# Inverse roots of the variances in the later projections: one power operation on GpSimd for ScalarE's root and VectorE's reciprocal

## What is computed

```python
def layer_norm(x, w, b, eps):
    mu = jnp.mean(x, axis=-1, keepdims=True)
    var = jnp.var(x, axis=-1, keepdims=True)
    return (x - mu) * jax.lax.rsqrt(var + eps) * w + b

xn = layer_norm(group_norm(x), w_in, b_in, eps)      # eps 1e-5, in layer 3 1e-6
p = (xn @ W_value + b_value) * sigmoid(xn @ W_gate + b_gate)
# layers 2 and 3 also: gate = sigmoid(xn @ W_ogate + b_ogate), stored for the end of the layer
```

## Time and profile before

| | before |
|---|---|
| median of 3 runs | 1588.93 us (1588.11 to 1591.24) |
| the profiled execution | 1591.19 us, of which the span is 1589.4 us |
| PE busy | 1357.7 us (85%) |
| DVE busy | 1217.4 us (77%) |
| ACT busy | 978.3 us (62%) |
| POOL busy | 447.3 us (28%) |
| L910, reciprocal, DVE | 12 of 3.35 us |
| L826, root, ACT | 12 of 0.72 us |
| table loads in the projections, ACT | 5 of 1.28 us (L843 2, L830 2, L836 1) |

### The profile page before, as it was taken

One profiled execution on the slowest core, in us unless ns is written; L12 is line 12 of the kernel. 1 busy time (PEld: TensorE's weight loads), 2 busy tenths in 40 slices (PEclk: granted clock), 3 DMA queues, 4 the chain that ended last, 5 costly groups with the idle time before them and its releaser, 6 DMA issues. The chain is left out here.

```text
span 1589.4 us, 26467 instructions
## 1 busy us (share of the span) xinstructions
PE 1357.7 (85%) x9025; PEld 750.7 (47%) x9025; DVE 1217.4 (77%) x2069; ACT 978.3 (62%) x1578; POOL 447.3 (28%) x387
## 2 busy tenths in 40 slices
PE   5767797878796997799979998898889979995987
PEld 5516332222583442345559997222245537772443
DVE  5644787699699886789957777997689968997664
ACT  4675588634344787677846665356768856662555
POOL 5400397320000893310000000685320000002665
PEclk9898898999898998999989999898999989996999
DMA  9368210056785220489988886794168989996998
GB/s 352 121 193 298 92 54 1 1 160 199 257 291 199 94 80 1 144 293 342 339 314 305 302 305 229 273 375 173 38 267 343 345 326 382 418 401 212 381 392 313
DMA packets 152692, 381.60 MB, mean 240 GB/s; under 512 B 15728, under 2 KB 15984, under 8 KB 152432
## 3 DMA queue, kind: packets, MB, share of 16 engines
q1 hardware_dynamic: 140176, 356.64, 61.8%
q10 hardware_dynamic: 12384, 23.28, 3.9%
HBM read 191.11 MB, written 188.74 MB: 239 GB/s over the span
## 5 line engine op out<-in xcount | busy, mean ns | idle before, releaser
L1162 PE MATMUL banks<-work 128*128 128x256 f32 x1408 | 335.5, 386 | 21.8 <-DVE work L1233 11.9
L1162 PEld LDWEIGHTS banks<-work 128*128 128x128 f32 x1408 | 262.3, 195 | 68.5 <-issue 16.7
L714 PE MATMUL banks<-work,w 64*64 64x512 f32 x2048 | 265.4, 609 | 12.5 <-DVE work L941 9.7
L1514 POOL TENSOR_TENSOR xT<-xT,work 128x512 f32<-128x512 f32 x192 | 241.0, 1271 | 60.0 <-DVE work L1563 56.6
L941 DVE SCALAR_TENSOR_TENSOR work<-banks,bias,work 128x512 f32<-128x512 f32 x256 | 188.5, 748 | 39.7 <-PE banks L714 33.0
L830 ACT ACTIVATE work<-banks,bias 128x512 f32<-128x512 f32 x256 | 171.7, 685 | 57.8 <-PE banks L714 57.7
L1192 ACT COPY work<-banks 128x512 f32<-128x512 f32 x176 | 103.1, 586 | 145.2 <-PE banks L1162 141.6
L714 PEld LDWEIGHTS banks<-work,w 64*64 64x64 f32 x2048 | 105.0, 135 | 129.7 <-DVE work L941 80.2
L1331 POOL MEMSET work<- 32x2048 bf16 x4 | 7.2, 1799 | 563.6 <-issue 466.7
L1259 DVE TENSOR_TENSOR work<-work 128x512 f32<-128x512 f32 x176 | 120.9, 687 | 58.3 <-ACT work L1192 57.2
L1563 DVE SCALAR_TENSOR_TENSOR work<-banks,bias,work 128x512 f32<-128x512 f32 x192 | 141.9, 747 | 30.2 <-ACT work L1488 15.1
(11 more groups left out here) (168 smaller groups left out, 2161.9 us busy)
## 6 DMA issues: line engine op xcount, KB each, us to landing
hidden_rows<-work SPq DMA_DIRECT2D x128, 512.0 KB, 4.0
work<-hidden_rows SPq DMA_DIRECT2D x120, 512.0 KB, 6.8
products<-work SPq DMA_DIRECT2D x88, 512.0 KB, 4.0
work<-products SPq DMA_DIRECT2D x88, 512.0 KB, 5.0
work<-gate_rows SPq DMA_DIRECT2D x64, 512.0 KB, 5.7
work<-hidden SPq DMA_DIRECT2D x40, 512.0 KB, 6.1
work<-in_x SPq DMA_DIRECT2D x32, 512.0 KB, 4.7
gate_rows<-work SPq DMA_DIRECT2D x32, 512.0 KB, 3.3
```

Of the source, the lines that this page charges most:

```text
L714: mm = pe.matmul(out[side, :], w(name)[rows, side], h[rows, t % H, :], start=True, stop=True)
L1162: mm = pe.matmul(ZB[c % 2][:, r * N:r * N + N], a[:, kk, rows_of(r, c)], x[:, kk, :], start=(kk == 0), stop=(kk == 1))
L1514: pool.tensor_tensor(columns(t), columns(t), term[:, t % RING, :], ALU.add).then_inc(x_sb, 1)
```

## The change

For each set, ACT's root and DVE's reciprocal are left out. The epsilon is added on DVE together with the clipping at zero (L905), and GpSimd raises the result to the power -0.5 with one `tensor_tensor` of 128x512, whose second input is the column of -0.5 read again for each column. GpSimd waits for the variance and for its own split of the set before. The dummy root that loads the table is left out too. The same holds for layers 1, 2 and 3. Left out of the diff below are the lines that drop the semaphore `sd_sb`.

```diff
--- before.py
+++ after.py
@@ -821,10 +821,6 @@
-            def root(x):
-                act.wait_ge(var_sb, 2 * x + 2)
-                nc.scalar.activation(sd[:, x % 2, :], sd[:, x % 2, :], ACT.Sqrt, bias=eps).then_inc(sd_sb, 1)
-
@@ -840,19 +836,14 @@
-            nc.scalar.activation(core.fold[:, 14:15], core.cols[:, 0:1], ACT.Sqrt)
             act.wait_ge(norm.gmean_in, 1)
             for u in range(PAIRS):
                 for x in range(SETS_OF_ROOTS - 2):
                     if u == 2 * last_step(x) + 4:
                         square_of_mean(x)
-                    if u == 2 * last_step(x) + 7:
-                        root(x)
                 squares(u)
             for x in (SETS_OF_ROOTS - 2, SETS_OF_ROOTS - 1):
                 square_of_mean(x)
-            for x in (SETS_OF_ROOTS - 2, SETS_OF_ROOTS - 1):
-                root(x)
@@ -876,6 +867,9 @@
             for x in range(SETS_OF_ROOTS):
                 rest = sd[:, x % 2, :]
+                pool.wait_ge(var_sb, 2 * x + 2)
+                at_least(pool, split, 4 * x)
+                pool.tensor_tensor(rec, rest, core.cols[:, 2:3].broadcast_to([P, T]), ALU.pow).then_inc(rec_sb, 1)
                 pool.wait_ge(rec_sb, x + 1)
                 pool.tensor_scalar(high[:, 0, :], rec, later[0], None, ALU.mult).then_inc(split, 1)
@@ -902,12 +896,7 @@
                 dve.wait_ge(var_sb, 2 * x + 1)
-                dve.tensor_scalar(var, var, 0.0, None, ALU.max).then_inc(var_sb, 1)
-
-            def inverse(x):
-                dve.wait_ge(sd_sb, x + 1)
-                at_least(dve, split, 4 * x)
-                dve.reciprocal(rec, sd[:, x % 2, :]).then_inc(rec_sb, 1)
+                dve.tensor_scalar(var, var, 0.0, eps, ALU.max, ALU.add).then_inc(var_sb, 1)
@@ -954,8 +943,6 @@
                     if u == 2 * last_step(x) + 5:
                         variance(x)
-                    if u == 2 * last_step(x) + 8:
-                        inverse(x)
                 squares(u)
@@ -978,8 +965,6 @@
-                if u in (2, 4):
-                    inverse(SETS_OF_ROOTS - 3 + u // 2)
```

More of the change, by code:

```diff
@@ L694, in project @@
         norm = GroupNorm(core, layer, f"proj{layer}", [n for n in (gate_w, value_w, ogate_w) if n], sums_w)
-        (sq_a, sq_v, sum_mm, mean_sb, var_sb, sd_sb, rec_sb, split, fac_mm, h_sb, gate_mm, val_mm, gate_sb,
-         val_sb) = core.sems(f"proj{layer}", "sq_a sq_v sum_mm mean_sb var_sb sd_sb rec_sb split fac_mm h_sb gate_mm "
+        (sq_a, sq_v, sum_mm, mean_sb, var_sb, rec_sb, split, fac_mm, h_sb, gate_mm, val_mm, gate_sb,
+         val_sb) = core.sems(f"proj{layer}", "sq_a sq_v sum_mm mean_sb var_sb rec_sb split fac_mm h_sb gate_mm "
                              "val_mm gate_sb val_sb")
```

## The result

| | before | after |
|---|---|---|
| median | 1589.5 us (4 runs) | 2205.6 us (4 runs, 2203.8 to 2208.4) |
| ratio | | 1.389 (95% interval 1.387 to 1.391) |
| span of the profiled execution | 1589.4 us | 2203.8 us |
| projection of layer 1 | 140.0 us | 383.8 us |
| projection of layer 2 | 204.7 us | 390.3 us |

A projection is measured here from DVE's first reduction (L580) to the table load on ACT that opens the next stage. The three grow by 613.5 us together, the span by 614.4 us: all of the loss lies in them.

What follows compares the result with a forecast made beforehand. No engine is full in the sums, where order decides; DVE, or DVE and PE in turn, pace the main loops. 6Q - 56 at Q = 24 us gives +88 us, hence 1677 us; range 1548 to 2060 us.

Steps and rivals of the forecast that it cites:

- Q: Length of one 128x512 power on GpSimd, run twelve times; estimated at 24 us, break-even at 9.3 us.
- The sum: All terms over three layers: 6Q - 26.6 - 24 - 5.5 = 6Q - 56 us, +88 us at Q = 24 us.
- first to fourth variance: Sums stage: 15.2 + 2Q us a layer against 72.2 us together before; 6Q - 26.6, floor about -13 us.
- late sets: Main loops: set 3 is needed after 70 or 128 us; two powers and splits, 2Q + 11.6, lie beyond that.
- rival 3: GpSimd's power without overlap of columns, Q over 45 us: 2058 us at 68, about 3500 at 192; chance 0.27.
- In the main loops: Without the reciprocals of sets 2 and 3, holes in the gate activations' steps vanish: 24 us gained over three layers.
- In front of the first gated product: Between fourth variance and first gated product, root and table load go: 1.9, 1.5 and about 2 us, 5.5 together.
- Start of the power: GpSimd's first power waits for two DVE squares after the first variance: 2.3 us added.
- Two waits: PE's first factors wait for split 0, DVE's fourth variance for split 1; main loop starts after two powers and splits.
- The clipping with the epsilon: Epsilon as one more operand in DVE's L905 of 0.43 us: at most 0.3 us, counted as nothing.
- Rival 1: GpSimd's power costs near its other elementwise work, Q under 9.3 us: faster, 1546 us at Q = 1.2; chance 0.21.
- Rival 4: DVE's squares shut out during power 0, set 1's variance late: up to 4 us a layer; no chance given.

Runs made afterwards that it cites:

- widths run: Kernel before, plus extra GpSimd multiplications and powers of 1 to 128 columns in layer 1's main loop; only its rows are used, 0.159 us for each further power column.
- one multiplication: Changed kernel with one multiplication of the same shape in place of GpSimd's power, so no inverse root is made; 1545.6 us, ratio 0.974.
- run with one activation: Kernel before with ScalarE's Abs_reciprocal_sqrt in place of root and reciprocal, written into the two buffers of the squared means; 1552.0 us, ratio 0.978.
- batched run: Kernel before, two reciprocal buffers, sets 2 and 3 by ScalarE's logarithms then exponentials, sets 0 and 1 by root and reciprocal; 1575.7 us, ratio 0.9925.

## Why the prediction was wrong

*The step that failed is the price of the power.* The prediction bounds a column between 2.3 ns and 0.37 us and takes an eighth of the upper end, 47 ns and Q = 24 us. The widths run measured 0.159 us a column, 0.43 of the upper end; Q is 82 us, 3.4 times the Q of the forecast. "Overlap shortens this" was the wrong part of the reasoning: a column costs the same 0.16 us from 1 to 512 columns, and the one-column row was within a factor of 2.3 of the answer. Its excess over a copy, 0.37 us, was 0.22 us of once-only cost over a multiplication's 0.19 us, and 0.16 us for the column. "Break-even wants 20 columns in flight" was right as a warning; the choice between the ends should have leaned on the row of the same operation, not toward the geometric mean.

*The sum held, at small Q by some luck.* It was tried at four lengths of Q. The traces give its two parts too: the way from the first to the fourth variance, and the way from there to the stage's end, both against the kernel before and summed over three layers.

| Q in the run | sum | measured | first to fourth variance: sum, trace | behind it: sum, trace |
|---|---|---|---|---|
| 1.2 us | -42 | -43 | -13, -16.4 | -29.5, -28.9 |
| 10.0 us | +4 | +5 | +33.4, +27.8 | -29.5, -24.6 |
| 22.2 us | +77 | +76 | +106.6, +100.3 | -29.5, -26.1 |
| 82 us, with the late sets | 492 - 56 + 106 + 95 = +637 | +616 | +465.4, +458.2 | +171.3, +156.4 |

The measured column is from medians and the traces are single executions, so the parts of a row needn't add up to it closer than some us. The late sets at 82 us go by rival 3's own rule: 2 x 82 + 11.6 = 175.6 us against 70 and 128 us. Rival 3 (Q over 45 us, chance 0.27) is what happened, in the part of it above 68 us to which the prediction gave 0.17. The direction (slower, chance 0.76) was right, and the range fell short, because its upper end was laid at Q = 68 us.

*Point by point.*
- In the main loops: 24 us. With one multiplication the holes are gone. The run with one activation gives 24.0 us for it, the batched run 19.8 us.
- In front of the first gated product, 5.5 us: the run with a multiplication has it and the run with one activation has not. They gain 43 and 35 us. Behind the fourth variance their traces gain 28.9 and 24.0 us, so the term measures 4.9 us; the other 2.7 us by which they differ lie ahead of the fourth variance.
- Start of the power: the prediction puts 2.3 us of squares ahead of it. After, the power starts 0.07 us behind the clipping, and two squares beside it take 3.25 us instead of 2.47 us; later ones keep 1.28 us. From the first to the fourth variance it is 176.8 = 2 x 82.4 + 11.9 us and not 15.2. With the powers 0.4 us longer than 82 us that makes 7 of the 21 us by which the sum is too high at 82 us.
- Late sets: this is where most of the rest lies. From the fourth variance to the stage's end the three layers take 99.7, 43.1 and 42.5 us more than with one multiplication, 185.3 us, where the sum has 200.8. The room for two powers and splits in a main loop was 76 us in layer 1 and 133 us in the others, and not 70 and 128 (in layer 1: 88.9 us with one multiplication, less the 12.9 us that stand behind the last split).
- Two waits: both ended at GpSimd's split, the fourth variance's with 84.72 us. PE's wait for the first factors is 73.24 us in layer 1.
- The clipping with the epsilon: 0.49 us instead of 0.43 us.
- Rival 1 (a power near the price of other elementwise work) is out by a factor of nearly 80: 81.95 us against 1.04 us for a multiplication of the same shape. The Trainium skill's account of two-input work (GPSIMD Engine Reference, 3.1 Elementwise — side-by-side cycle accounting), about 2.6 cycles an element, does not carry over to the power.
- Rival 4 (DVE shut out) did not happen. The Trainium skill (SBUF — State Buffer, SBUF: two separate sides) says that the port pair is held for the whole instruction. The trace disagrees for a power: squares with two SBUF inputs (1.28 and 1.29 us) and a clipping (0.49 us) run at their usual length inside an instruction of 82 us. Only at its start is there a hold-up: the two squares there take 0.8 us longer and the power 0.97 us. For multiplications the rows agree with a hold-up (12.49 us instead of 8.93 us).

## What to carry to other kernels

Price an operation by what it costs per column, from two widths; a row of one column bounds it from above, and where no second width exists, stay near that bound rather than halfway to another operation's price. A chain that moves to an idle engine is still a chain: what it costs is its length times the number of steps that stand in front of a wait (here two powers a layer), and more once the later steps outlast the work that covers them; and the break-even length (9.3 us) can be had before the price is known. If the gain is in freeing one engine, look for the engine that does the same in one instruction: one activation of 0.72 us, in the root's place, took the reciprocal off VectorE and gave 35 us.

## What the runs showed of the hardware

- GpSimd's power costs 0.41 us and 0.159 us a column (10.53 us for 64 columns, 81.95 us for 512), the same with 32 or 128 partitions, with the bases 1.7 and 1.0, and with a column read again or a full second input; a multiplication 0.19 us and 1.7 ns a column (1.04 us for 512).
- While a power runs, VectorE's squares (1.28 us) and clippings (0.49 us) from SBUF keep their length, apart from its start (3.25 us for two squares instead of 2.47 us); beside multiplications they do not (1.08 us instead of 0.49 us for a clipping).
- Logarithm and exponential cost a table load of 1.28 us at each change in this program. The absolute value's reciprocal root shares a table with the square and not with the sigmoid: no load stands between the first two, and one of 1.28 us ahead of the sigmoid.
